# Attention outputs made transposed, a step later, and scaled by spread inverses

## The chip, the cores and the metric

The kernel runs on one core of a Trainium2 chip. What is measured is the time on the device of one execution, in microseconds (us); a lower time is better. TensorE is written PE in the profile, its weight loads PEld, VectorE is DVE, ScalarE is ACT, GpSimd is POOL, and SyncE, which issues most transfers, is SP.

## The reference

Eight sequences of 512 tokens by 128 features go through two residual layers. Layer 0 is a state space filter (16 states, 256 inner channels) with a gate and feed-forward part behind it, beside a two-of-eight expert layer chosen for each sequence. Layer 1 is causal attention with 16 heads of 64, beside an expert layer in which each token picks two of eight experts. The part that matters here is the attention:

```
q, k = _rope(q, k)
scores = jnp.einsum('bhqd,bhkd->bhqk', q, k)
scores = jnp.where(causal[None, None], -jnp.inf, scores)
attn = jax.nn.softmax(scores / math.sqrt(DK), axis=-1)
out = jnp.einsum('bhqk,bhkd->bhqd', attn, v)
out = out.transpose(0, 2, 1, 3).reshape(Bx, Sx, H * DV)
return out @ wo.T + bo
```

where v carries a bias bv. All data are float32.

## The kernel before

Each engine has an instruction list of its own; they meet through semaphores. The eight sequences go through in laps. A lap of sequence b has a `phase_1` (the filter's tail and layer 0 of b, the token experts of b-1, the front of the filter of b+1) and a `phase_2` (the attention of b, and beside it 13 of the 16 states of the filter's scan of b+1). The last sequence's `phase_2` has no scan beside it, since there is no b+1.

`phase_2` has 32 steps. The heads are taken in eight pairs j, and each pair in four steps t = 0 to 3, one for each block of 128 query rows; step s = 4j + t treats tiles n = 2s and 2s+1, the pair's two heads. A query block t sees t+1 key blocks. For each tile the work goes from engine to engine:

- PE, `scores` (L1038, with the causal mask added by L1041). The two heads' keys and queries lie in partitions 0 to 63 and 64 to 127. A step makes the scores of step s+2.
- DVE, `largest` (L1856): the row maxima. ACT, `exponentials` (L1341): exp and the row sums.
- PE, `turn` (L1049): transposes the exponentials into the bank G[2], t+1 blocks. There is one such bank, so the next turn waits for the copy out of it.
- ACT, `copy_turned` (L1349): copies them to PT, of which there are two, one for each head.
- PE, `weigh_values` (L1064): stationary is the turned block (128 by 128), moving are 64 columns of V; the output in G[3] has queries in partitions. Each float32 matmul shows as two weight loads and two matmuls.

Per pair, in step t = 0 of the next pair, DVE's `divide` inverts the row sums (L1861) and multiplies all of G[3] by them (L1868). In step t = 1 (`OUT_STEP`) PE's `turn_out` (L1073) transposes the result in four blocks into the bank FC, and ACT's `copy_out` (L1359) adds bv and puts it where `project_out` (L1081) reads it at the end of the phase. The last pair's `turn_out` stands behind the first seven `project_out`.

PE's order in a step is: turn(2s), weigh(2s-1), the scan's two selections (L796 and L800, `PICKS_AT`), turn(2s+1), a guest that uses FC (a projection L1026, `turn_out`, or rows to be turned), and then scores(s+2) and weigh(2s). DVE's order is: the maxima of step s+1, `divide` if t = 0, the scan's parts of this step (`PIECES`: a product L1550, a scan L1555, a product L1577), and a projection's rotation (L1850).

Of the kernel before, what the change touches and what calls it, by code (L numbers as in the profile page):

```python
# [35 lines left out]
P = 128  # L36
# [87 lines left out]
def build(nc, xT, weights, vecs, conv_rows, dt_w, a_log, moe, experts,  # L124
          row_biases, cos, sin, identity, causal, row_of, in_u_w, outT):
    ctx = ExitStack()
    with ctx:
# [77 lines left out]
        def reg(k):  # L205
# [10 lines left out]
        PT = REG[:, 16:18, :]  # L216
# [31 lines left out]
        s_alog = ctx.enter_context(nc.semaphore("alog_exp"))  # L248
# [81 lines left out]
        ot_mm = signal("ot_mm", PAIRS)  # L330
        ot_copy = signal("ot_copy", PAIRS)
# [48 lines left out]
                 d1_mm, d2_mm, lg_mm, wb_mm, e1_mm, e2_mm, v_mm, pj_mm, sc_mm, pt_mm, pv_mm, ot_mm, wo_mm, gl_mm,  # L380
                 xtok_mm, rank_mm, xt_mm, gg_mm, ug_mm, dn_mm, yt_mm] + [n.by_pe for n in norms]
        by_act = [biased, u_silu, r_silu, soft, da_exp, qsq_d, ksq_d, q_gelu, g_act, d1_gelu, rt_act,
                  e1_gelu, v_copy, p_exp, pt_copy, ot_copy, gt_act, sl_act, xtok_c, xt_copy, yo_copy] + [n.s_square for n in norms]
# [113 lines left out]
        for s_ in range(STEPS):  # L497
            j_, t_ = s_ // TILES, s_ % TILES
            if s_ < 2:
                guest[s_] = (("proj", 2 + s_), (biased, 3 + s_))  # L500
            if t_ in PROJECT_AT and j_ + 2 < PAIRS:
                m_ = 2 * (j_ + 2) + PROJECT_AT.index(t_)
                guest[s_] = (("proj", m_), (biased, m_ + 1))
            if t_ == OUT_STEP and j_:
                guest[s_] = (("out", j_ - 1), (ot_copy, j_))
# [179 lines left out]
        def _(pe):  # L685
# [366 lines left out]
            def weigh_values(b, n):  # L1052
                j, i = n // PER_PAIR, n % PER_PAIR
                h, t = tile_of(n)
                pe.wait_ge(pt_copy.sem, pt_copy.at(b, n + 1))
                if i == 0 and j:

                    pe.wait_ge(o_d.sem, o_d.at(b, j))
                elif i == 0:
# [8 lines left out]
            def turn_out(b, j):  # L1068

                pe.wait_ge(o_d.sem, o_d.at(b, j + 1))  # L1070
                bank = take(b, ("out", j))
                for t in range(TILES):
                    mm = pe.transpose(bank[:, t * P:(t + 1) * P], O[:, t * P:(t + 1) * P], ident[:, :])  # L1073
                mm.then_inc(ot_mm.sem, 1)

            def project_out(b, j):
                if j == 0:

                    pe.wait_ge(p_exp.sem, p_exp.at(b))
                pe.wait_ge(ot_copy.sem, ot_copy.at(b, j + 1))  # L1080
                pe.matmul(G[4][:, :], w("wo", j * D), ot_slot(j), start=j == 0, stop=j == PAIRS - 1,  # L1081
                          skip_group_check=True).then_inc(wo_mm.sem, 1)
# [7 lines left out]
            def attention_end(b, following):  # L1090
                project_out(b, PAIRS - 1)

                pe.wait_ge(p_exp.sem, p_exp.at(b))
                pe.wait_ge(ot_copy.sem, ot_copy.at(b))
                pe.wait_ge(gt_d.sem, gt_d.at(b))
# [4 lines left out]
            def phase_2(b, f, t):  # L1100
# [17 lines left out]
                for s in range(STEPS):  # L1118
# [3 lines left out]
                    if s:  # L1122
                        weigh_values(b, 2 * s - 1)
# [10 lines left out]
                    if key[0] == "proj":  # L1134
                        project(b, key[1])
                    elif key[0] == "out":
                        turn_out(b, key[1])
# [30 lines left out]
            def late():  # L1168

                pe.wait_ge(s_late, n_late)  # L1170
                pe.wait_ge(s_made, 17)
# [9 lines left out]
        def _(act):  # L1181
# [109 lines left out]
            def token_use(b, part, i, following):  # L1291
# [6 lines left out]
                if i >= 2:  # L1298
                    act.wait_ge(hh_d.sem, hh_d.at(b, i - 1))
                act.activation(SL[:, i % 2, :], G[2 * (i % 2)][:, :], ACT.Tanh, scale=0.5).then_inc(sl_act.sem, 1)  # L1300
# [43 lines left out]
            def copy_turned(b, n):  # L1344
                width = (tile_of(n)[1] + 1) * P
                act.wait_ge(pt_mm.sem, pt_mm.at(b, n + 1))
                if n >= 2:
                    act.wait_ge(pv_mm.sem, pv_mm.at(b, n - 1))
                act.activation(PT[:, n % 2, 0:width], G[2][:, 0:width], ACT.Copy).then_inc(pt_copy.sem, 1)  # L1349

            def copy_out(b, j):
                if j == 0:

                    act.wait_ge(wo_mm.sem, wo_mm.at(b - 1))
                    act.wait_ge(dn_mm.sem, dn_mm.at(b - 1))
                    act.wait_ge(e2_mm.sem, e2_mm.at(b))
                    act.wait_ge(yf_d.sem, yf_d.at(b))
                act.wait_ge(ot_mm.sem, ot_mm.at(b, j + 1))
                act.activation(ot_slot(j), ring_bank[("out", j)][:, :], ACT.Identity, bias=vec("bv", j)).then_inc(ot_copy.sem, 1)  # L1359
# [8 lines left out]
            def phase_2(b, f, t):  # L1368
# [10 lines left out]
                for s in range(STEPS):  # L1379
# [13 lines left out]
                    if s + 1 < STEPS:  # L1393
                        exponentials(b, 2 * s + 3, f)
                    if key[0] == "proj":
                        add_bias(b, key[1])
                    elif key[0] == "out":
                        copy_out(b, key[1])
# [20 lines left out]
        def _(dve):  # L1419
# [439 lines left out]
            def divide(b, j):  # L1859
                dve.wait_ge(p_exp.sem, p_exp.at(b, PER_PAIR * (j + 1)))  # L1860
                dve.reciprocal(rows[:, j % 2, 1, :], rows[:, j % 2, 0, :]).then_inc(rec_d.sem, 1)  # L1861
                if j:

                    dve.wait_ge(ot_mm.sem, ot_mm.at(b, j))
                dve.wait_ge(pv_mm.sem, pv_mm.at(b, PER_PAIR * (j + 1)))
                dve.wait_ge(rec_d.sem, rec_d.at(b, j + 1))

                dve.tensor_tensor(O.rearrange("p (t h d) -> p t h d", t=TILES, h=2),  # L1868
                                  G[3][:, :].rearrange("p (t h d) -> p t h d", t=TILES, h=2),
                                  rows[:, j % 2, 1, :].rearrange("p (h t) -> p t h", h=2).unsqueeze(3).to_broadcast([P, TILES, 2, DK]),  # L1870
                                  ALU.mult).then_inc(o_d.sem, 1)
# [12 lines left out]
            def phase_2(b, f, t):  # L1884
# [13 lines left out]
                for s in range(STEPS):  # L1898
# [5 lines left out]
                    if t_ == 0 and j:  # L1904
                        divide(b, j - 1)
# [13 lines left out]
                    elif key[0] == "return" and t is not None:  # L1919
                        give_back(t, ring_bank[key])  # L1920
                divide(b, PAIRS - 1)
# [12 lines left out]
            def late():  # L1934
# [6 lines left out]
                dve.wait_ge(s_made, 17)  # L1941
# [233 lines left out]
```

## Time and profile before

| | |
|---|---|
| median of 3 runs | 2456.86 us (2449.41 to 2474.56) |
| the profiled execution | 2465.26 us, its span 2463.1 us |
| PE, DVE, ACT, POOL busy | 83%, 67%, 48%, 39% of the span |
| mean granted clock of PE | 0.913 |

The profile is of one execution. The busy share of PE contains the modelled tail of each matmul, so a busy PE can still be one that waits.

### The profile page before, as it was taken

Reading aid. Unit: us, or ns where it says so; the run is one execution under the profiler, and the core shown is the slowest. Engines: PE = TensorE matmul, PEld = TensorE weight load, DVE = VectorE, ACT = ScalarE, POOL = GpSimd, SP = SyncE. Lnnn points to the kernel's source line nnn. Section 1 sums busy time; section 2 is a strip of 40 time slices with the busy share of each in tenths; the row PEclk is TensorE's granted clock in tenths of the full one; section 3 lists DMA queues with packets and bytes.
Section 4 is the critical chain, followed back from the end, with each engine's and each line's share of the span. In section 5 each row is a group of like instructions: output and inputs, shape, how many; then the busy total and the mean of one; then the engine's idle time right before and its main releaser. Section 6 shows DMA issues by size and latency. Waiting matters only on the chain.

```text
span 2463.1 us, 38971 instructions
## 1 busy us (share of the span) xinstructions
PE 2051.6 (83%) x11640; PEld 1426.4 (58%) x11640; DVE 1661.6 (67%) x2938; ACT 1186.9 (48%) x2703; POOL 955.0 (39%) x580
## 2 busy tenths in 40 slices
PE   4267888987899888998899888998889878888985
PEld 1043556755666556665566656665656646666664
DVE  4945886578855888558965688558876688645431
ACT  2223564345634466345643466345653456424631
POOL 1420572037710476007920287105940177203501
PEclk8577899998999899999999999999999999989997
DMA  2000012321213112321123112221123211232233
GB/s 105 0 18 0 35 51 70 115 70 41 85 65 111 57 44 69 105 99 44 57 71 115 68 48 81 78 98 62 46 74 106 87 44 60 72 125 71 71 107 119
DMA packets 82452, 175.06 MB, mean 71 GB/s; under 512 B 11448, under 2 KB 42560, under 8 KB 81984
## 3 DMA queue, kind: packets, MB, share of 16 engines
q1 hardware_dynamic: 78144, 164.05, 19.4%
q0 software_dynamic: 4096, 8.40, 1.1%
q8 instruction: 107, 1.75, 0.3%
q14 instruction: 105, 0.86, 0.1%
HBM read 123.71 MB, written 15.14 MB: 56 GB/s over the span
## 4 chain that ended last, share of the span: by engine, by line
PE 49%; DVE 21%; issue 14%; ACT 6%; POOL 5%; DMA 3%; SPq 1%; DVEq 1%; ACTq 0%; POOLq 0%
PE G L1064 7%; DVE HS L1555 6%; PE G L1049 5%; PE FM L1038 3%; PE G L953 3%; PE FC L1026 3%; PE G L942 3%; PE G L936 3%; DMA MW<-moe 2%; ACT REG L1349 2%; PE G L1081 2%; PE FM L906 2%; DVE maxes L1856 2%; DVE D L1550 2%; POOL Y L1984 2%
## 5 line engine op out<-in xcount | busy, mean ns | idle before, releaser
L1064 PEld LDWEIGHTS G<-REG 128*128 128x128 f32 x2560 | 347.5, 198 | 59.5 <-issue 49.7
L1555 DVE TENSOR_TENSOR_SCAN HS<-DA,D 128x1024 f32<-128x1024 f32 x128 | 359.3, 2807 | 19.4 <-ACT DA L1226 18.9
L1064 PE MATMUL G<-REG 128*128 128x64 f32 x2560 | 356.0, 272 | 3.2 <-DVE REG L1868 3.2
L1049 PE MATMUL G<-ident,REG 128*128 128x128 f32 x1280 | 241.7, 289 | 113.3 <-ACT REG L1349 111.1
L1984 POOL TENSOR_TENSOR Y<-Y,HC 128x1024 f32<-128x1024 f32 x114 | 271.1, 2378 | 163.4 <-DVE HC L1577 120.8
L1349 ACT ACTIVATE REG<-G 128x128 f32<-128x128 f32 (+3 forms) x512 | 222.9, 435 | 110.6 <-PE G L1049 105.0
L1995 POOL TENSOR_TENSOR REG<-REG,cos_t 128x512 f32<-128x512 f32 x128 | 170.8, 1334 | 257.1 <-ACT REG L1325 257.0
L1049 PEld LDWEIGHTS G<-ident,REG 128*128 128x128 f32 x1280 | 148.7, 149 | 162.1 <-issue 127.1
L1341 ACT ACTIVATE REG<-G,maxes 128x128 f32<-128x128 f32 (+3 forms) x384 | 195.4, 509 | 82.1 <-DVE maxes L1856 82.1
L1998 POOL TENSOR_TENSOR REG<-REG 128x512 f32<-128x512 f32 x128 | 207.1, 1618 | 56.9 <-DMA REG<-ROT 49.0
L1038 PE MATMUL G<-REG 64*128 64x128 f32 (+3 forms) x768 | 217.4, 482 | 9.8 <-POOL REG L1998 8.8
L1226 ACT ACTIVATE DA<-DELTA,a_neg 128x511 f32<-128x511 f32 x256 | 180.1, 718 | 46.8 <-DVE HS L1555 46.7
L1856 DVE TENSOR_REDUCE maxes<-G 128x1 f32<-128x128 f32 (+3 forms) x384 | 166.0, 458 | 14.2 <-PE G L1041 13.1
L936 PE MATMUL G<-XGT,MW 128*128 128x128 f32 x960 | 139.4, 292 | 29.1 <-DMA MW<-moe 28.9
L936 PEld LDWEIGHTS G<-XGT,MW 128*128 128x128 f32 x960 | 129.6, 204 | 56.2 <-issue 49.4
L1962 POOL TENSOR_SCALAR Y<-US,V_ 128x512 f32<-128x512 f32 x16 | 24.8, 1560 | 351.6 <-ACT US L1200 351.6
L1550 DVE TENSOR_TENSOR D<-DU,FB 128x1024 f32<-128x1024 f32 x114 | 138.2, 1213 | 23.6 <-PE FB L796 21.0
L1289 ACT ACTIVATE YO<-G 128x128 f32<-128x128 f32 x120 | 33.1, 276 | 247.6 <-PE G L953 247.6
L1968 POOL TENSOR_TENSOR DU<-DELTA,US 128x1024 f32<-128x1024 f32 x8 | 18.8, 2346 | 333.6 <-DVE DELTA L1542 333.6
L942 PEld LDWEIGHTS G<-XGT,MW 128*128 128x128 f32 x960 | 129.4, 204 | 24.0 <-issue 24.0
L1325 ACT ACTIVATE REG<-FC,V_ 128x512 f32<-128x512 f32 x112 | 77.0, 687 | 134.0 <-DVE ROT L1850 132.7
L953 PE MATMUL G<-MW,HC 128*128 128x128 f32 x960 | 140.0, 294 | 1.1 <-DVE HC L1732 1.1
(291 smaller groups left out, 4267.1 us busy)
## 6 DMA issues: line engine op xcount, KB each, us to landing
MW<-moe SPq DMA_DIRECT2D x120, 768.0 KB, 4.2
REG<-ROT SPq DMA_DIRECT2D x256, 128.0 KB
EW<-experts SPq DMA_DIRECT2D x16, 514.5 KB, 4.6
XG<-x_rows SPq DMA_DIRECT2D x8, 960.0 KB, 5.4
y_rows<-YO SPq DMA_DIRECT2D x120, 64.0 KB, 1.5
X<-xT SPq DMA_DIRECT2D x8, 256.0 KB, 6.2
W<-weights SPq DMA_DIRECT2D x1, 2048.0 KB, 9.4
REG<-xT SPq DMA_DIRECT2D x8, 256.0 KB, 2.9
```

Of the source, the lines that this page charges most:

```text
L936: mm = pe.matmul(G[2 * (i % 2)][:, c * P:(c + 1) * P], MW[:, i % SLOTS, c * P:(c + 1) * P], XGT[:, i, :], start=True, stop=True)
L942: mm = pe.matmul(G[2 * (i % 2) + 1][:, c * P:(c + 1) * P], MW[:, i % SLOTS, at:at + P], XGT[:, i, :], start=True, stop=True)
L953: mm = pe.matmul(G[4][:, 0:D], HH[:, i % 4, c * P:(c + 1) * P], MW[:, i % SLOTS, 2 * HID + c * D:2 * HID + (c + 1) * D], start=c == 0, sto ...
L1038: pe.matmul(bank[:, 0:width], QK[lo:lo + DK, j % 2, 0, t * P:(t + 1) * P], QK[lo:lo + DK, j % 2, 1, 0:width], start=True, stop=False)
L1049: mm = pe.transpose(G[2][:, c * P:(c + 1) * P], PR[:, n % 2, c * P:(c + 1) * P], ident[:, :])
L1064: mm = pe.matmul(G[3][:, col:col + DK], PT[:, n % 2, c * P:(c + 1) * P], V[:, c, j * P + h * DK:j * P + (h + 1) * DK], start=c == 0, stop= ...
L1341: act.activation(PR[:, n % 2, 0:width], ring_bank[("score", n)][:, 0:width], ACT.Exp, bias=maxes[:, j % 2, at:at + 1], accum_out=rows[:, j ...
L1349: act.activation(PT[:, n % 2, 0:width], G[2][:, 0:width], ACT.Copy).then_inc(pt_copy.sem, 1)
L1555: dve.tensor_tensor_scan(HS[:, :, :].rearrange("p h s -> p (h s)"), DA[:, n % 2, :, :].rearrange("p h s -> p (h s)"), D1[:, :, :].rearrang ...
L1856: dve.tensor_reduce(maxes[:, j % 2, at:at + 1], ring_bank[("score", n)][:, 0:width], AX.X, ALU.max, negate=True).then_inc(nm_d.sem, 1)
L1984: pool.tensor_tensor(Y[:, :, :], Y[:, :, :], HC_EARLY if early else HC[:, n % 2, :, :], ALU.add).then_inc(y_add.sem, 1)
L1998: pool.tensor_tensor(rotated, rotated, REG[:, 8 + m % 2, :], ALU.add).then_inc(rope_d.sem, 1)
```

## The change

PE's `weigh_values` now makes the output transposed. Stationary are 64 columns of V, moving is the turned block with 128 columns, and the output of head h lies in partitions 64h to 64h+63 of G[3]. Both heads of a step are done together, alternating, one step later than the first was before: in step s behind turn(2s), the values of step s-1. PT has a second pair of buffers (SL, which is free in this phase). `turn_out` is replaced by `spread_inverse`: eight matmuls whose stationary operand is a column of inverses repeated 64 times and whose moving one is the identity, so that the inverses stand beside the transposed outputs; for the last pair it comes ahead of the `project_out`s. ACT copies G[3] to O in step t = 0 of the next pair, and DVE multiplies O by the spread inverses in step t = 1, right behind the maxima of that step and ahead of the scan's parts. The value bias goes through wo into bo once, in `late`.

```
-            def weigh_values(b, n):
...
-                col = t * P + h * DK
-                for c in range(t + 1):
-                    mm = pe.matmul(G[3][:, col:col + DK], PT[:, n % 2, c * P:(c + 1) * P],
-                                   V[:, c, j * P + h * DK:j * P + (h + 1) * DK], start=c == 0, stop=c == t)
-                mm.then_inc(pv_mm.sem, 1)
+            def weigh_values(b, s):
+                j, t = s // TILES, s % TILES
+                pe.wait_ge(pt_copy.sem, pt_copy.at(b, 2 * s + 2))
+                if t == 0 and j:
+                    pe.wait_ge(o_copy.sem, o_copy.at(b, j))
+                elif t == 0:
+                    pe.wait_ge(place_d.sem, place_d.at(b, 5))
+                for c in range(t + 1):
+                    for h in range(2):
+                        mm = pe.matmul(G[3][h * DK:(h + 1) * DK, t * P:(t + 1) * P], V[:, c, j * P + h * DK:j * P + (h + 1) * DK],
+                                       PT[s % 2][:, h, c * P:(c + 1) * P], start=c == 0, stop=c == t)
+                        if c == t:
+                            mm.then_inc(pv_mm.sem, 1)
+            def spread_inverse(b, j):
+                pe.wait_ge(rec_d.sem, rec_d.at(b, j + 1))
+                bank = take(b, ("out", j))
+                for t in range(TILES):
+                    for h in range(2):
+                        mm = pe.matmul(bank[h * DK:(h + 1) * DK, t * P:(t + 1) * P],
+                                       rows[:, j % 2, 1, h * TILES + t:h * TILES + t + 1].to_broadcast([P, DK]), ident[:, :],
+                                       start=True, stop=True)
+                mm.then_inc(rinv_mm.sem, 1)
...
                     turn(b, 2 * s)
                     if s:
-                        weigh_values(b, 2 * s - 1)
+                        weigh_values(b, s - 1)
...
-                    if t_ == 0 and s + 2 < STEPS:
+                    if s + 2 < STEPS:
                         scores(b, s + 2)
-                    weigh_values(b, 2 * s)
-                    if t_ and s + 2 < STEPS:
-                        scores(b, s + 2)
-                weigh_values(b, N_TILES - 1)
+                weigh_values(b, STEPS - 1)
+                spread_inverse(b, PAIRS - 1)
                 for j in range(PAIRS - 1):
                     project_out(b, j)
-                turn_out(b, PAIRS - 1)
...
+                for j in range(PAIRS):
+                    mm = pe.matmul(G[2][:, 0:1], w("wo", j * D), vec("bv", j), start=j == 0, stop=j == PAIRS - 1)
...
             def copy_out(b, j):
+                if j:
+                    act.wait_ge(o_d.sem, o_d.at(b, j))
+                act.wait_ge(pv_mm.sem, pv_mm.at(b, PER_PAIR * (j + 1)))
+                act.activation(O, G[3][:, :], ACT.Copy).then_inc(o_copy.sem, 1)
...
+            def divide(b, j):
...
+                dve.wait_ge(o_copy.sem, o_copy.at(b, j + 1))
+                dve.wait_ge(rinv_mm.sem, rinv_mm.at(b, j + 1))
+                dve.tensor_tensor(ot_slot(j), O, ring_bank["out", j][:, :], ALU.mult).then_inc(o_d.sem, 1)
...
                     if t_ == 0 and j:
-                        divide(b, j - 1)
+                        invert_sums(b, j - 1)
+                    if key[0] == "out":
+                        divide(b, key[1])
```

## Rows read from the trace of the kernel before

**Rows 1.** The page: busy time, and the chain that ended last by engine.

```profile
PE 2051.6 (83%) x11640; PEld 1426.4 (58%) x11640; DVE 1661.6 (67%) x2938; ACT 1186.9 (48%) x2703; POOL 955.0 (39%) x580
...
PE 49%; DVE 21%; issue 14%; ACT 6%; POOL 5%; DMA 3%; SPq 1%; DVEq 1%; ACTq 0%; POOLq 0%
```

**Rows 2.** Windows: a lap's attention with scan, and the last lap's without.

```profile
core 0: us, PE busy (x) PEld busy (x) DVE busy (x) ACT busy (x) POOL busy (x), PEclk, DMA share, GB/s
1130.00:1267.00 137.00, 115.11 (x774) 81.96 (x773) 119.78 (x147) 89.99 (x244) 102.40 (x61) 0.96 0.17 58
...
2286.00:2362.00 76.00, 71.10 (x523) 53.36 (x522) 31.38 (x66) 53.89 (x153) 34.52 (x30) 1.00 0.22 76
```

**Rows 3.** The waits in 1130 to 1267: who for whom, total, times, longest.

```profile
PE G L1049 <- ACT REG L1349: 16.2, 20, 3.4
...
DVE maxes L1856 <- PE FM L1041: 4.0, 5, 0.9
DVE REG L1868 <- PE G L1064: 3.3, 6, 1.8
```

**Rows 4.** The chain that ended last, 1130 to 1267, shares by line.

```profile
by line: issue 23.5%; PE G L1064 12.1%; DVE HS L1555 8.4%; PE G L1049 7.7%; DVE maxes L1856 5.0%; ACT REG L1349 4.8%; PE FM L1038 4.5%; PE FC L1026 4.4%; DVE HC L1577 3.4%; DVE place_i L1832 2.6%; PE G L1038 2.0%; DVE ROT L1850 1.9%; POOL R
```

**Rows 5.** The timeline, PE and PEld, around a group of scores.

```profile
1251.40 0.97 PEld L1064 LDWEIGHTS G<-REG 128*128 128x128 f32 x8
...
1252.45 0.48 PE L1038 MATMUL FM<-REG 64*128 64x256 f32 x1
1252.45 0.48 PE L1038 MATMUL G<-REG 64*128 64x256 f32 x1
...
1252.77 0.38 PE L1038 MATMUL FM<-REG 64*128 64x256 f32 x1
...
1253.08 0.10 PEld L1041 LDWEIGHTS FM<-causal_bf,ident_bf 128*128 128x128 bf16 x1 [0.33 <-issue]
```

**Rows 6.** The timeline at a matmul that fills eight columns of the array.

```profile
466.82 0.75 PEld L953 LDWEIGHTS G<-MW,HC 128*128 128x128 f32 x6
467.69 0.10 PEld L765 LDWEIGHTS FM<-US,W 128*8 128x8 f32 x2
```

**Rows 7.** The chain in order of time in the last lap (start, us, what).

```profile
2287.40 0.39 ACT REG L1349
2287.80 0.14 issue
...
2288.78 0.39 PE G L1064 x4
...
2292.84 0.61 PE G L1064 x6
...
2294.57 0.61 ACT REG L1349
...
2296.80 0.84 PE G L1064 x8
...
2298.60 0.84 PE G L1064 x8
```

**Rows 8.** The timeline at two `turn_out`s, DVE's maxima beside them.

```profile
1242.27 1.01 DVE L1856 TENSOR_REDUCE maxes<-G 128x1 f32<-128x384 f32 x2
1243.32 0.47 PEld L1073 LDWEIGHTS FC<-ident,REG 128*128 128x128 f32 x4
...
1257.37 1.01 DVE L1856 TENSOR_REDUCE maxes<-G 128x1 f32<-128x384 f32 x2
1257.93 0.47 PEld L1073 LDWEIGHTS FC<-ident,REG 128*128 128x128 f32 x4
```

**Rows 9.** The timeline at the end of an attention phase, and L714's loads.

```profile
1266.99 0.69 DVE L1868 TENSOR_TENSOR REG<-G,rows 128x512 f32<-128x512 f32 x1 [1.84 <-PE G L1064]
...
1274.07 0.30 PEld L1081 LDWEIGHTS G<-REG,W 128*128 128x128 f32 x2 [1.01 <-ACT REG L1359]
...
1298.13 1.87 PEld L714 LDWEIGHTS FM<-ones,REG 128*128 128x128 f32 x16
```

More of the change, by code:

```diff
@@ L215, in build @@
         PR = REG[:, 14:16, :]
-        PT = REG[:, 16:18, :]
+        PT = (REG[:, 16:18, :], SL)
         O, OT = reg(18), reg(19)
@@ L329, in build @@
         o_d = signal("o_d", PAIRS)
-        ot_mm = signal("ot_mm", PAIRS)
-        ot_copy = signal("ot_copy", PAIRS)
+        rinv_mm = signal("rinv_mm", PAIRS)
+        o_copy = signal("o_copy", PAIRS)
         wo_mm = signal("wo_mm", PAIRS)
@@ L504, in build @@
             if t_ == OUT_STEP and j_:
-                guest[s_] = (("out", j_ - 1), (ot_copy, j_))
+                guest[s_] = (("out", j_ - 1), (o_d, j_))
             if s_ == RETURN_STEP:
@@ L1136, in phase_2 @@
                     elif key[0] == "out":
-                        turn_out(b, key[1])
+                        spread_inverse(b, key[1])
                     elif key[0] == "turn":
@@ L1299, in token_use @@
                     act.wait_ge(hh_d.sem, hh_d.at(b, i - 1))
+                else:
+                    act.wait_ge(pv_mm.sem, pv_mm.at(b))
                 act.activation(SL[:, i % 2, :], G[2 * (i % 2)][:, :], ACT.Tanh, scale=0.5).then_inc(sl_act.sem, 1)
@@ L1346, in copy_turned @@
                 act.wait_ge(pt_mm.sem, pt_mm.at(b, n + 1))
-                if n >= 2:
-                    act.wait_ge(pv_mm.sem, pv_mm.at(b, n - 1))
-                act.activation(PT[:, n % 2, 0:width], G[2][:, 0:width], ACT.Copy).then_inc(pt_copy.sem, 1)
-            def copy_out(b, j):
[L1352 to L1359, printed above, removed]
+                if n >= 4:
+                    act.wait_ge(pv_mm.sem, pv_mm.at(b, n - 3))
+                elif n >= 2:
+                    act.wait_ge(hh_d.sem, hh_d.at(b - 1))
+                act.activation(PT[n // 2 % 2][:, n % 2, 0:width], G[2][:, 0:width], ACT.Copy).then_inc(pt_copy.sem, 1)
+            def copy_out(b, j):
+                if j:
+                    act.wait_ge(o_d.sem, o_d.at(b, j))
+                act.wait_ge(pv_mm.sem, pv_mm.at(b, PER_PAIR * (j + 1)))
+                act.activation(O, G[3][:, :], ACT.Copy).then_inc(o_copy.sem, 1)
             def early_scan(f, n, part, b):
@@ L1394, in phase_2 @@
                         exponentials(b, 2 * s + 3, f)
+                    if s and s % TILES == 0:
+                        copy_out(b, s // TILES - 1)
                     if key[0] == "proj":
                         add_bias(b, key[1])
-                    elif key[0] == "out":
-                        copy_out(b, key[1])
                     elif key[0] == "turn":
@@ L1857, in largest, with invert_sums @@
                                   negate=True).then_inc(nm_d.sem, 1)
-            def divide(b, j):
+            def invert_sums(b, j):
                 dve.wait_ge(p_exp.sem, p_exp.at(b, PER_PAIR * (j + 1)))
                 dve.reciprocal(rows[:, j % 2, 1, :], rows[:, j % 2, 0, :]).then_inc(rec_d.sem, 1)
[L1862 to L1871, printed above, removed]
+            def divide(b, j):
+                if j == 0:
+                    dve.wait_ge(wo_mm.sem, wo_mm.at(b - 1))
+                    dve.wait_ge(dn_mm.sem, dn_mm.at(b - 1))
+                    dve.wait_ge(e2_mm.sem, e2_mm.at(b))
+                dve.wait_ge(o_copy.sem, o_copy.at(b, j + 1))
+                dve.wait_ge(rinv_mm.sem, rinv_mm.at(b, j + 1))
+                dve.tensor_tensor(ot_slot(j), O, ring_bank["out", j][:, :], ALU.mult).then_inc(o_d.sem, 1)
             def attention_end(b, following):
@@ L1920, in phase_2 @@
                         give_back(t, ring_bank[key])
+                invert_sums(b, PAIRS - 1)
                 divide(b, PAIRS - 1)
@@ L1940, in late @@
                 dve.tensor_scalar(q_b, q_b, DK ** -0.5, None, ALU.mult).then_inc(s_made, 1)
-                dve.wait_ge(s_made, 17)
+                dve.wait_ge(s_alog, 3)
+                dve.tensor_tensor(vec("bo"), vec("bo"), G[2][:, 0:1], ALU.add).then_inc(s_made, 1)
+                dve.wait_ge(s_made, 18)
             def finish(t):
```

23 lines of the change are left out of this document (7 added, 16 removed).

## The prediction

> **What bounds the kernel now.** I read the page first [rows 1]: PE is busy 83% and carries 49% of the chain that ended last, DVE 67% and 21%. That is an average, so next I cut out one lap's attention by windows [rows 2]. In its 137 us DVE is busy 119.8 and PE 115.1. The last lap's attention, which has no scan beside it, is a different machine: in 76 us PE is busy 71.1 and DVE only 31.4. So PE sets the last lap, and the seven laps with a scan are bound by PE and DVE together, each waiting for the other at times. The list of waits says at what [rows 3]: PE's turns wait 16.2 us for ACT's copies in 20 places, DVE's maxima wait 4.0 us for scores, and `divide` waits 3.3 us for the values. The chain of such a lap gives the matmuls of the values (L1064) 12.1%, or 16.6 us of the 137 [rows 4]. Those matmuls take 0.11 us apiece (0.97 us for a run of eight loads [rows 5]) and a lap has 320 (16 heads, ten blocks, two matmuls each), so 35 us of PE; 16.6 of 35 is 0.47, and with that share of PE's time I convert a saving on PE into one of the lap.
>
> **The change part by part.**
>
> *The values.* The count of matmuls stays 320 a lap. Moving 128 columns instead of 64 costs nothing by itself: four loads and matmuls of L1073, which move 128 columns, take 0.47 us, which is the same 0.11 apiece [rows 8]. The gain can only be that the two heads' matmuls, which fill different columns of the array, go at once. No row of this kernel shows that. The nearest rows are the scores, whose heads fill different rows of the array: both start at 1252.45, and the second of a head starts 0.32 later [rows 5]. If columns behave as rows do, a step with n matmuls takes n/2 places of 0.11 us; if not, n. The bounds are far apart, and I take the half, since the scores are the nearest row.
>
> *Changing the shape.* The same rows price it. The eight loads from 1251.40 would be followed by a ninth at 1252.28 or so, and the first of the scores comes at 1252.45: 0.15 lost. The pair that starts at 1252.77 streams 256 columns in 0.21 (0.32 less a load of 0.11), ends at 1252.98, and the next load comes at 1253.08, 0.10 late and with nothing to cover it, another 0.05 [rows 5]. At L765, which fills eight columns, six loads from 466.82 should be followed at 467.48 and are at 467.69 [rows 6]: 0.21 lost, so partial columns pay it too. In and out cost 0.30 us, once a step.
>
> The Trainium skill, in "TensorEngine Tiling (Array Packing)", Key Properties, says both things: different tiles can load and multiply in parallel, and a change of the tiling mode drains the engine. The trace agrees with the second (the 0.10 to 0.21 above); with the first it agrees for rows and is silent for columns.
>
> *One pair of heads on PE, by the last lap's chain* [rows 7]. Between turn(2s) and turn(2s+1) PE must wait for ACT's copy: 0.39 us for t = 1 to 0.61 for t = 3 and 0.14 of passing on. In t = 0 it is the eight matmuls of the values that take longer, 0.84. These gaps are 0.55, 0.64, 0.75, 0.84 for t = 1, 2, 3, 0 (the copy of t = 2 lies between the two shown). After the change the gap holds the values of the whole step before: 2, 4, 6, 8 places of 0.11 and 0.30, so 0.52, 0.74, 0.96, 1.18. It grows by 0, 0.10, 0.21, 0.34: 0.65 us. Behind turn(2s+1) the second head's values go: 0.39, 0.61, 0.84 [rows 7] and 0.22 for t = 0, 2.06 us. What stands there still (scores, and a projection in two steps of four) is longer than the next copy, so I count no new wait; it costs up to 0.4 us in a step if ACT is late with it. `spread_inverse` has 16 matmuls in 8 places, 0.88, and a change of shape, 0.15 (its way out is shared with the scores behind it), where `turn_out` took 0.44: 0.6 more. Sum: 0.65 + 0.6 - 2.06 = -0.8 us for a pair, -6.5 us for a lap.
>
> *The end of the phase.* Before, the last `turn_out` and ACT's copy stand between the seventh `project_out` and the eighth, and PE waits 1.01 us for it [rows 9]. Now the spreading comes ahead of six microseconds of `project_out`, which cover ACT's copy and DVE's product. That takes 1.0 us off each lap.
>
> *DVE.* The product stays 0.69 us [rows 9] and one is made for each pair, so DVE has no less to do. The wait changes. Before, `divide` waits 3.3 us in a lap, of which 1.84 lie at the end beside `project_out` [rows 3, 9], so 1.5 on the way. After, DVE stands behind the maxima of step t = 1 until PE has come to the spreading in that same step and done it, and behind it wait the scan's parts, so the product with B or C that PE's selections and POOL's sums wait for. Two places show how DVE and PE stand there: the maxima end at 1243.28 and 1258.38, and `turn_out` begins at 1243.32 and 1257.93 [rows 8]. The spreading would end some 1.2 us behind that beginning (0.15, 0.88, the tail of the last matmul 0.17 or so), so DVE waits 1.2 and 0.8: 1.0 a pair, 7 in a lap, less the 1.5 that go: +5.5 us of waiting. What of it is paid runs from nothing (PE is quicker, DVE falls behind it and finds the inverses made) to all of it. I take a third, 1.8 us, because DVE's own lines that show on the chain (8.4, 5.0, 3.4, 2.6 and 1.9%) make 21% of it beside the 12.1% of the values alone [rows 4], and because the maxima's own wait for the scores, 4.0 us [rows 3], takes up part of a late start.
>
> *ACT, POOL, SP.* ACT copies G[3] as often as it copied FC before. It moves from t = 1 to t = 0 and stands behind the exponentials there; PE needs it a step later. No transfer is moved. The values wait for both copies of a step that is over, so nothing is queued behind them that isn't free already.
>
> *`late`.* Eight matmuls of one column show as sixteen, 1.87 us by L714's [rows 9], and one small operation on DVE: 2.2 us, once.
>
> *Sum.* A lap with a scan: 0.47 of -6.5 is -3.1, with -1.0 and +1.8 that is -2.3; seven of them -16.1. The last lap: -6.5 - 1.0 = -7.5. `late` +2.2. Together -21.4 of the profiled 2465.3 us, 0.87%. The profiled execution lies 0.3% above the median, 2456.86; the same share of that gives 2436 us.
>
> **The rivals.**
>
> *PE's saving is paid out in full.* If DVE's waits are all for PE's sake and shrink with it, each scan lap gains 7.5 us: 7 x 7.5 + 7.5 - 2.2 = 58 us, 2399. For it: DVE waits for scores and values at all. Against it: DVE is busy 119.8 of 137 us, so more than 17 us a lap isn't there for anyone.
>
> *DVE's wait takes it.* All 5.5 us of waiting are paid and PE's saving beside DVE is worth only the 1.0 at the end: 7 x 4.5 - 7.5 + 2.2 = +26 us, 2483. It decides from the point where PE reaches the spreading later than DVE ends its maxima; both rows seen have it so. Halfway lies no change, 2460.
>
> *The columns don't go at once (slower).* Then the gaps behind turn(2s) hold 4, 8, 12, 16 places and 0.30: 0.74, 1.18, 1.62, 2.06 against 0.55, 0.64, 0.75, 0.84, 2.8 us more; the spreading is 1.76 + 0.15 - 0.44 = 1.5 more; 2.06 are saved. That is +2.2 a pair and 17.8 a lap. The last lap: +16.8. A scan lap: 0.47 x 17.8 - 1.0 + a third of (7 x 1.9 - 1.5) = +11.3, seven +79. With `late` +98 us, 4%: 2555. For it speaks that each float32 stream reads 128 partitions, where each of the scores' reads 64; nothing in the trace shows two full streams at once.
>
> *Only the loads get in each other's way.* The two heads' matmuls overlap, and each load waits for the matmul before it, so that a place is 0.16 (0.11 and half of a 128-column load, 0.05). Twenty places in a pair's values and eight in the spreading add 1.4 us to the -0.8: +0.6 a pair and +4.8 a lap. The last lap: +3.8; a scan lap: 0.47 of 4.8, -1.0 and the third of DVE's wait, +1.8 to +2.2, together +3.2. With `late` +28 us, 2485. "TensorE: Matmul & The Clock Gate", What overlaps and what doesn't, of the Trainium skill says that a load overlaps a matmul in flight only where the row group differs, and here it doesn't. The trace speaks against it in the full shape: the eight loads of L1064 come at 0.11 with matmuls between them in the same rows [rows 5].
>
> **How the numbers follow.** A measurement of this kernel tells 1% from no change, 25 us. Chances: my sum with its unknowns, 2405 to 2465, 0.47; PE's saving in full, 2370 to 2405, 0.08; DVE's wait or the loads, 2465 to 2500, 0.20; the columns one after the other, 2500 to 2590, 0.25. From 2395 to 2545 hold some 0.8 of it. Faster by over 1% (below 2432) takes the second and a little over half of the first: 0.34. Slower by over 1% (above 2481) takes the last and a small part of the third: 0.30. The rest, 0.36, is within 1%.
>
> **What will show it.** In the profile after, L1064's successor for the two heads starts in pairs a few nanoseconds apart if the columns go at once, and a step with 16 of them takes 0.9 and not 1.8 us. The wait of DVE's product for the spreading is 1 us a pair. PE's turns wait far less for ACT's copies than the 16.2 us a lap of before. The last lap's attention is 7 us shorter, a scan lap's 2. The wait ahead of the eighth `project_out` is gone. I am wrong if the pairs don't start together, if a change of shape costs other than 0.15 us, or if the scan laps move otherwise than the sum of both engines' waits.

## The result, and the profile after

The changed kernel takes 2484.28 us (median of 20 runs, 2470.26 to 2501.34) where the kernel before takes 2461.58 us (median of 20 beside them). The ratio is 1.009, with a 95% interval of 1.0068 to 1.0112: it is slower by 0.9%, where I had forecast 0.9% faster. The profiled execution has a span of 2480.3 us at a granted clock of 0.906.

The page of the kernel after, its busy line and the chain by engine, which answer to [rows 1]:

```profile
PE 2036.6 (82%) x12424; PEld 1294.5 (52%) x12424; DVE 1612.0 (65%) x2939; ACT 1174.2 (47%) x2703; POOL 939.6 (38%) x580
...
PE 47%; DVE 19%; issue 17%; POOL 7%; ACT 6%; DMA 3%; SPq 1%; DVEq 0%; ACTq 0%; POOLq 0%
```

PE does less (2036.6 us for 2051.6), DVE too, and the kernel takes longer. So it waits more. The groups of instructions of the kernel after say where (busy, mean ns of one, idle time ahead of it and what ended it):

```profile
L1049 PE MATMUL G<-ident,REG 128*128 128x128 f32 x1280 | 245.6, 292 | 137.8 <-ACT SL L1361 79.0 <-ACT REG L1361 55.5 <-issue 0.6
L1564 DVE TENSOR_TENSOR_SCAN HS<-DA,D 128x1024 f32<-128x1024 f32 x128 | 330.1, 2579 | 14.5 <-ACT DA L1232 13.2
L1065 PE MATMUL G<-REG 128*64 128x128 f32 x1024 | 88.2, 294 | 23.6 <-ACT REG L1368 21.3 <-issue 1.0
L1880 DVE TENSOR_TENSOR EW<-REG,FC 128x512 f32<-128x512 f32 x32 | 22.0, 688 | 61.0 <-PE FC L1077 51.2 <-issue 9.8
L1880 DVE TENSOR_TENSOR MW<-REG,FC 128x512 f32<-128x512 f32 x24 | 16.5, 687 | 36.3 <-PE FC L1077 36.3
L1880 DVE TENSOR_TENSOR REG<-REG,FC 128x512 f32<-128x512 f32 x8 | 5.5, 687 | 17.9 <-PE FC L1077 17.9
```

Three readings. DVE's product (L1880) waits 61.0 + 36.3 + 17.9 = 115 us, where `divide` waited 28 in the run before (3.3 in the stretch of [rows 3]). PE's turns (L1049) wait 134.5 us for ACT's copies, where they waited 111.1 (16.2 in the stretch). And the first values of a pair wait 21.3 us for a copy that wasn't in that place before, ACT's of G[3] (L1368). One place of the timeline of the kernel after shows how they come about (start, duration, engine, line, idle time before):

```profile
889.68 0.60 ACT L1368 ACTIVATE REG<-G 128x512 f32<-128x512 f32 x1
889.82 1.22 DVE L1586 TENSOR_TENSOR HC<-HS,FB 128x1024 f32<-128x1024 f32 x1
890.42 0.44 PE L1065 MATMUL G<-REG 128*64 128x128 f32 x4 [0.53 <-ACT REG L1368]
890.96 1.02 DVE L1865 TENSOR_REDUCE maxes<-G 128x1 f32<-128x384 f32 x2
891.10 0.39 PE L796 MATMUL FB<-S,pick 96*128 96x512 bf16 x1 [0.24 <-DVE HC L1586]
891.33 0.38 PE L1049 MATMUL G<-ident,REG 128*128 128x128 f32 x2
891.64 1.09 PE L1077 MATMUL FC<-ident,rows 128*64 128x128 f32 x16
892.86 0.69 DVE L1880 TENSOR_TENSOR EW<-REG,FC 128x512 f32<-128x512 f32 x1 [0.88 <-PE FC L1077]
```

PE comes to the values at 889.9 and stands 0.53 us, since ACT copies G[3] behind the exponentials; then it stands for the scan's selection; the spreading begins at 891.64 and ends 1.1 us later. DVE ended its maxima at 891.98 and waits 0.88. This is one of the shortest of these waits. Over the seven laps with a scan they are 1.8 us a pair in the mean; the first pair of a lap waits 2.5 us or more, in two laps 4.1.

### The profile page after: what moved, and what is told of

The parts are those of the page before. It is cut to its first block, busy times and chain, and to the rows that moved or that the text cites. A ratio compares the mean times of both kernels' runs of the same rounds, so it can differ in the third digit from the quotient of the medians.

```text
span 2480.3 us, 40604 instructions
## 1 busy us (share of the span) xinstructions
PE 2036.6 (82%) x12424; PEld 1294.5 (52%) x12424; DVE 1612.0 (65%) x2939; ACT 1174.2 (47%) x2703; POOL 939.6 (38%) x580
## 3 DMA queue, kind: packets, MB, share of 16 engines
q8 instruction: 114, 1.87, 0.3%
## 4 chain that ended last, share of the span: by engine, by line
PE 47%; DVE 19%; issue 17%; POOL 7%; ACT 6%; DMA 3%; SPq 1%; DVEq 0%; ACTq 0%; POOLq 0%
DVE HS L1564 4%; PE G L1049 4%; PE G L1065 4%; DMA MW<-moe 3%; PE G L942 3%; PE G L936 2%; PE G L953 2%; PE FC L1077 2%; PE FC L1026 2%; PE G L1087 2%; POOL Y L1998 2%; PE FM L906 2%; PE FM L1038 2%; POOL REG L2012 2%; POOL REG L2009 2%
## 5 line engine op out<-in xcount | busy, mean ns | idle before, releaser
L1049 PE MATMUL G<-ident,REG 128*128 128x128 f32 x1280 | 245.6, 292 | 137.8 <-ACT SL L1361 79.0
L1564 DVE TENSOR_TENSOR_SCAN HS<-DA,D 128x1024 f32<-128x1024 f32 x128 | 330.1, 2579 | 14.5 <-ACT DA L1232 13.2
L1049 PEld LDWEIGHTS G<-ident,REG 128*128 128x128 f32 x1280 | 150.4, 148 | 183.3 <-issue 130.6
L2012 POOL TENSOR_TENSOR REG<-REG 128x512 f32<-128x512 f32 x128 | 185.5, 1449 | 59.9 <-DMA REG<-ROT 52.6
L1361 ACT ACTIVATE SL<-G 128x256 f32<-128x256 f32 (+1 forms) x256 | 126.5, 494 | 43.9 <-PE G L1049 41.4
L1361 ACT ACTIVATE REG<-G 128x128 f32<-128x128 f32 (+1 forms) x256 | 97.7, 382 | 94.6 <-PE G L1049 92.7
L953 PEld LDWEIGHTS G<-MW,HC 128*128 128x128 f32 x960 | 134.2, 213 | 14.7 <-issue 13.9
```

The costliest lines, as they stand in the source:

```text
L953: mm = pe.matmul(G[4][:, 0:D], HH[:, i % 4, c * P:(c + 1) * P], MW[:, i % SLOTS, 2 * HID + c * D:2 * HID + (c + 1) * D], start=c == 0, sto ...
L1049: mm = pe.transpose(G[2][:, c * P:(c + 1) * P], PR[:, n % 2, c * P:(c + 1) * P], ident[:, :])
L1361: act.activation(PT[n // 2 % 2][:, n % 2, 0:width], G[2][:, 0:width], ACT.Copy).then_inc(pt_copy.sem, 1)
L1564: dve.tensor_tensor_scan(HS[:, :, :].rearrange("p h s -> p (h s)"), DA[:, n % 2, :, :].rearrange("p h s -> p (h s)"), D1[:, :, :].rearrang ...
L2012: pool.tensor_tensor(rotated, rotated, REG[:, 8 + m % 2, :], ALU.add).then_inc(rope_d.sem, 1)
```

## The experiments

All times are ratios to the kernel before, run beside each. The kernel after stands at 1.009. Differences in us are differences of these ratios times 2462 us. The kernel before took 2462 to 2470 us beside the experiments, so where an expectation below gives a time, the ratio and not the bare time decides.

**Where DVE's product stands.** The product moves behind the scan's parts of its step:

```
-                    if key[0] == "out":
-                        divide(b, key[1])
...
                     if f is not None:
                         for n, part in PIECES[s]:
                             front_step(f, n, part)
+                    if key[0] == "out":
+                        divide(b, key[1])
```

> The kernel after, with DVE's product of a pair moved behind the scan's parts of step t = 1. Three theories share the 22 us that the kernel after is slower than before. A, DVE's wait: DVE stands at the product 105 us in the whole run and the scan's parts stand behind it. Then the wait here falls below 50 us and the time to about 2460 us, that of before. B, the cost on PE: sixteen matmuls and two changes of shape a pair, and nothing of the wait is paid. Then the wait falls but the time stays between 2475 and 2490 us. C, ACT's queue: the turns and the values wait for ACT's copies (134 and 21 us), and DVE's place changes nothing: 2475 to 2490 us too, with those two waits as before. Against A alone speaks one thing: the projection of step t = 2 writes the bank that the product frees, so PE may wait for a later product (up to 1 us a pair, some 50 us in all), and the time then stays near 2484.

Measured: 0.9952 (0.9926 to 0.9978), so 1.4%, 34 us, less than the kernel after. The wait at the product is 34 us in place of 115, and PE waits 7 us for the product at its projections. Theory A holds: 81 us less waiting go with 34 us less time, a share of 0.42. The share is not the price of the wait alone, since the turns wait 17 us less and DVE's scans take 27 us more here (their lengths are compared further down).

**Where PE's spreading stands.** It goes from behind turn(2s+1) to behind turn(2s) of the same step, ahead of the values:

```
                     turn(b, 2 * s)
+                    if key[0] == "out":
+                        spread_inverse(b, key[1])
                     if s:
                         weigh_values(b, s - 1)
...
-                    elif key[0] == "out":
-                        spread_inverse(b, key[1])
```

> The kernel after, with the spreading of the inverses moved on PE from behind turn(2s+1) to right behind turn(2s) in step t = 1, ahead of the values, so some 2 to 3 us earlier. A, DVE's wait: it falls by 1.5 us or more at each of 49 products, by over 60 us in all, and the time falls to about 2460 us. B, the cost on PE: PE does the same matmuls, so 2475 to 2490 us. C, ACT's queue: the spreading now covers PE's waits for the copy of G[3] (21 us) and of turn(2s), so those fall by 15 us or more, and the time falls by as much even if DVE's wait weren't paid: 2465 to 2475 us.

Measured: 0.9832 (0.9794 to 0.9871), 2433.24 us: 2.6%, 64 us, less than the kernel after, and 1.7% faster than before, which took 2470.29 us beside it. It is the best version that computes everything. The groups of this kernel:

```profile
L1049 PE MATMUL G<-ident,REG 128*128 128x128 f32 x1280 | 243.5, 291 | 106.4 <-ACT SL L1361 62.7 <-ACT REG L1361 40.3 <-ACT REG L1350 0.2
L1065 PE MATMUL G<-REG 128*64 128x128 f32 x1024 | 87.4, 293 | 0.7
```

Both A and C come out: DVE's wait is 48 us, the wait for the copy of G[3] is gone (the spreading fills it), and the turns wait 31 us less. The same matmuls in another place take off more than the whole loss, so B, that the loss is the cost on PE, is refuted. That the spreading costs PE something is another matter; the run with two of the sixteen, below, prices it.

**DVE's wait by itself, first try.** DVE multiplies by another table and doesn't wait:

```
-                dve.wait_ge(rinv_mm.sem, rinv_mm.at(b, j + 1))
-                dve.tensor_tensor(ot_slot(j), O, ring_bank["out", j][:, :], ALU.mult).then_inc(o_d.sem, 1)
+                dve.tensor_tensor(ot_slot(j), O, sin_t[:, :], ALU.mult).then_inc(o_d.sem, 1)
```

> The kernel after, where DVE multiplies the copied outputs by the table of sines in SBUF in place of the spread inverses and doesn't wait for PE there; PE still spreads them. The outputs are not divided by the sums of their exponentials. It prices the wait for PE by itself. A: without the wait the scan laps lose all that they had gained by it, 2455 us or less (a third of the 105 us of waiting, or more). B and C: 2475 to 2490 us. What stands there may be taken up by the wait for the scores or the copy of G[3] behind it; then the wait at the product goes and DVE's other waits rise by most of it.

Measured: 1.0032 (1.0011 to 1.0053), 0.6% or 14 us less than the kernel after. That is neither A's 29 us or more nor the nothing of B and C, and the trace says why the run answers another question. Its view of that line (duration ns minimum, median, maximum):

```profile
L1879 DVE TENSOR_TENSOR EW<-REG,sin_t x32: 682/1118/4115, 296.9 to 2330.4; 128x512 f32<-128x512 f32 x32
L1879 DVE TENSOR_TENSOR MW<-REG,sin_t x24: 682/2139/4099, 363.6 to 2368.8; 128x512 f32<-128x512 f32 x24
```

The product, 0.69 us with one operand in PSUM, takes up to 4.1 us with both in SBUF. I had changed two things at once.

> As the run without DVE's wait, and PE does two of the sixteen matmuls that spread the inverses. It leaves the change of shape and takes 0.77 us of PE's time from each of 64 pairs, 49 us in all. The outputs are not divided by the sums of their exponentials. A: within 5 us of the run without the wait in the scan laps, 6 us less in the last lap: 2445 to 2455 us. B, the cost on PE: 25 to 49 us less than the run without the wait. C: as A, no more than 10 us less.

In the same version PE does only two of the sixteen (`for t in range(1)`). Measured: 0.9958 (0.9936 to 0.998), 0.74% or 18 us less than the one above, for 49 us of PE's time: a share of 0.37. It lies between A's 11 (5 and the last lap's 6) and B's 25, so the sixteen matmuls are not free, though they are not what makes the change slow.

**DVE's wait by itself, again.** DVE reads the bank FC as a guest left it, and PE writes its sixteen matmuls into a part of G[3] that is overwritten later (G[1] for the last pair). The outputs are not scaled by the inverses:

```
-                dve.wait_ge(rinv_mm.sem, rinv_mm.at(b, j + 1))
+                for of, k in ring_free["out", j]:
+                    if of is not o_d:
+                        dve.wait_ge(of.sem, of.at(b, k))
...
-                bank = take(b, ("out", j))
+                take(b, ("out", j))
+                bank = G[3] if j < PAIRS - 1 else G[1]
...
-                        mm = pe.matmul(bank[h * DK:(h + 1) * DK, t * P:(t + 1) * P],
+                        mm = pe.matmul(bank[h * DK:(h + 1) * DK, (2 + t % 2) * P:(3 + t % 2) * P],
```

> The run without DVE's wait used a table in SBUF, and the product then took 1.07 to 2.26 us in place of 0.69, which hid what was asked. Here DVE multiplies by what the bank FC last held, a read of PSUM as in the kernel after, and PE writes the same sixteen matmuls into a part of another bank that is overwritten later; DVE does not wait for them. The outputs are not divided by the sums of their exponentials. A: the wait of 105 us is gone but for the copies at the ends, the product takes 0.69 us, and the time falls by 34 us or more against the kernel after: 2450 us or less. If the wait is not what costs (B, C): 2475 to 2490 us.

Measured: 0.9927 (0.9899 to 0.9955), 1.6% or 40 us less than the kernel after. The product takes 0.68 us, and its wait, now for ACT, is 20 us in place of 115. So 95 us less waiting of DVE go with 40 us less time, again 0.42. PE's turns wait far less as well:

```profile
L1049 PE MATMUL G<-ident,REG 128*128 128x128 f32 x1280 | 243.0, 290 | 80.2 <-ACT SL L1362 51.5 <-ACT REG L1362 26.2 <-ACT REG L1351 0.2
```

That is 77.7 us for ACT's copies, where the kernel after has 134.5 and the kernel before 111.1. The turns' longer wait in the kernel after goes with DVE's wait: ACT's exponentials, which PE turns, wait 79 us for DVE's maxima here and 115 us in the kernel after.

**ACT's copy of G[3]** goes one instruction earlier:

```
+                    if s and s % TILES == 0:
+                        copy_out(b, s // TILES - 1)
                     if s + 1 < STEPS:
                         exponentials(b, 2 * s + 3, f)
-                    if s and s % TILES == 0:
-                        copy_out(b, s // TILES - 1)
```

> The kernel after, with ACT's copy of G[3] one instruction earlier, ahead of the second exponentials of step t = 0. C, ACT's queue: PE's wait for that copy at the first values of a pair, 21 us in all, goes, and the time falls by 10 to 20 us. A, DVE's wait: PE reaches the spreading up to 0.4 us earlier, so DVE's wait falls by 10 to 20 of its 105 us, and the time by 5 to 10 us. Against both: the exponentials, which both PE's next turn and the reciprocal wait for, come 0.6 us later in each pair, and the time stays within 5 us of the kernel after.

Measured: 1.0014 (0.9988 to 1.004), 0.75% or 19 us less. The wait for the copy falls from 21.3 to 4.8 us, DVE's only from 115 to 106. C holds for this wait. DVE's scans take 9 us less in this kernel, so some of the 19 may be theirs. The two gains, 40 and 19 us, make 59; the early spreading, which takes away most of both, gained 64.

**The order alone.** The kernel before with its own matmuls, and the values of both heads one step late (with the second buffers for the turned blocks):

```
                     turn(b, 2 * s)
                     if s:
+                        weigh_values(b, 2 * s - 2)
                         weigh_values(b, 2 * s - 1)
...
-                    if t_ == 0 and s + 2 < STEPS:
-                        scores(b, s + 2)
-                    weigh_values(b, 2 * s)
-                    if t_ and s + 2 < STEPS:
+                    if s + 2 < STEPS:
                         scores(b, s + 2)
```

> The kernel before, with its own matmuls (turned outputs, one head after the other, the product ahead of turn_out), where the values of both heads of a step go one step late behind turn(2s) and the copies have a second pair of buffers, as in the kernel after. It prices the order alone. If the late, bunched values are what costs (theory C: turns and G[3] wait longer for ACT), it is slower than before by 15 us or more, 2475 us or above. If the wait for the spreading is what costs (A), it is within 10 us of before, 2452 to 2472 us. By the lengths of the gaps behind turn(2s), which would hold 4 to 16 places of 0.11 us, PE does not save anything here, so no gain is expected from either.

Measured: 1.0104 (1.0063 to 1.0144), slower by as much as the whole change. But the reason isn't the one that I had written for it: its turns wait 102 us for ACT, less than before. What rises is `divide`'s wait for the last values, from 27.4 to 70.3 us, since both heads' values of step t = 3 now stand behind turn(2s) of t = 0, where DVE asks for them. By the trace it is DVE's wait once more, at another instruction; no run of this order without that wait was made.

**Both moves at once.**

> Both moves at once: the spreading right behind turn(2s), and DVE's product behind the scan's parts of its step. Each alone took time off the kernel after: 34 us and 64 us by the ratios. If they take away the same wait (A), the wait at the product goes from 48 us to the 20 at the phases' ends and the time stays within 8 us of the early spreading alone, 2425 to 2440 us. If each takes away something of its own, it is 2415 us or less. If a late product now holds back the projection of step t = 2, which writes the same bank (7 us of waiting with the product behind), it is above 2440 us.

Measured: 1.003 (0.9994 to 1.0067), 2.0% or 48 us worse than the early spreading alone, though the wait at the product is 20.6 us. A new cause had to be found. The timeline of this kernel, DVE's scan, GpSimd beside it, and PE:

```profile
911.12 6.19 DVE L1564 TENSOR_TENSOR_SCAN HS<-DA,D 128x1024 f32<-128x1024 f32 x1
...
911.58 2.35 POOL L1998 TENSOR_TENSOR Y<-Y,HC 128x1024 f32<-128x1024 f32 x1
913.89 1.26 POOL L2009 TENSOR_TENSOR REG<-REG,cos_t 128x512 f32<-128x512 f32 x1
915.31 3.06 POOL L2012 TENSOR_TENSOR REG<-REG 128x512 f32<-128x512 f32 x1 [0.16 <-POOL REG L2009]
...
918.99 0.30 PE L1049 MATMUL G<-ident,REG 128*128 128x128 f32 x1 [2.80 <-ACT REG L1361]
```

The scan, 2.3 us by itself, takes 6.19 where GpSimd has a sum of 2.35 us and a product of 1.26 in hand, both on SBUF, and the last of GpSimd's three takes 3.06 in place of 1.27. PE stands 2.8 us behind it. In this kernel pair 4 of a lap takes 16.6 us without such a meeting and 21.5 with it; from the first turn to the last, the laps with a scan take 132 or 140 us, but for the first with 137. The Trainium skill, "SBUF — State Buffer", Who interferes with whom, says that a DVE instruction with two SBUF inputs contends with a GpSimd instruction that reads SBUF, and that the second to issue is blocked. The trace agrees in which pairs of operations meet. As to the order, 50 scans of this kernel take over 2.6 us, and 45 of them start while one of GpSimd's sums or products already runs, which agrees; the one shown is of the other five, where the scan starts first, at 911.12, and is stretched even so. GpSimd's spans are rough, so these five decide nothing.

**Light GpSimd.** Four kernels (before, after, early spreading, both moves) where those sums and products of GpSimd touch 64 columns in place of 1024 or 512 (14 of the 128 sums keep their width). The other columns are left out, so the outputs are not the reference's:

```
+                w_ = S if early else 32
-                pool.tensor_tensor(Y[:, :, :], Y[:, :, :], ...
+                pool.tensor_tensor(Y[:, :, 0:w_], Y[:, :, 0:w_], ...
-                pool.tensor_tensor(rotated, rotated, cos_t[:, :], ALU.mult)
+                pool.tensor_tensor(rotated[:, 0:64], rotated[:, 0:64], cos_t[:, 0:64], ALU.mult)
...
```

> The kernel before, where GpSimd's sum into Y (2.36 us) and its two products and sums of the rotary embedding (1.27 us each) touch 64 of their 1024 or 512 columns, as many instructions and the same waits; so those sums are left out for the other columns. It asks what the stretched scans are worth: in the kernel before, DVE's scans take 2.3 us alone and 4 to 6.4 us where such an operation of GpSimd runs beside them, 65 us more in all. Theory P (the stretches, and which pairs they fall on, decide the differences of some 5 us between laps): all 112 scans of the attention laps take 2.3 us, the laps are alike within 1 us, and the time falls by 45 us or more. Rival: the scans are stretched by something else (DMA, ACT), and stay between 2.3 and 6 us; the time falls by no more than the 10 us for which PE waits for GpSimd.

> The kernel after with the same light GpSimd. P: scans of 2.3 us, even laps. Against the light kernel before: the kernel after had 37 us of stretched scans where before had 65 and was yet 22 us slower; if DVE's wait of 1.6 us a pair is simply paid, it is slower than the light before by 20 to 50 us. If the wait matters only where it moves the scan to GpSimd's operation, the two are within 10 us of each other, or after is the faster by up to 20.

> The kernel after with the early spreading and the light GpSimd. The early spreading gained 64 us on the kernel after. If that was PE's and DVE's waits, it is again 40 us or more faster than the light after. If half of it was the luck of where scans and GpSimd's operations met, it gains 15 to 35 us here.

> Early spreading, late product, and the light GpSimd. With GpSimd as it was, the late product made the early spreading 48 us slower, with stretched scans of 79 us against 47. P: that loss was the stretches, so here it is within 8 us of the light early spreading. Rival: the loss is in the waits of the products with B and C for PE's selections (64 us against 31), which come later behind a late PE; then it stays 25 us or more slower.

Measured, in that order: 0.9801 (0.9768 to 0.9833), 0.9918 (0.9888 to 0.9949), 0.9581 (0.9549 to 0.9613), 0.9583 (0.9548 to 0.9617). The scans of the light kernel before and of both moves:

```profile
L1555 DVE TENSOR_TENSOR_SCAN HS<-DA,D 128x1024 f32<-128x1024 f32 x128 | 297.4, 2324 | 19.8 <-ACT DA L1226 16.6 <-DVE D L1550 1.9 <-issue 0.6
```
```profile
L1564 DVE TENSOR_TENSOR_SCAN HS<-DA,D 128x1024 f32<-128x1024 f32 x128 | 297.7, 2326 | 14.2 <-ACT DA L1232 11.9 <-DVE D L1559 1.7
```

With light GpSimd the 128 scans take 297 us in every kernel. Against that, the heavy ones lose 62 us to the meetings in before (359.3), 33 in after, 43 with the early spreading (339.8) and 75 with both moves (372.0). The others stand between: 358 us of scans with the product behind, 338 without the wait, 321 with the copy ahead, 354 with the order alone. The loss of both moves is gone (0.9583 beside 0.9581), and the rival falls: the products with B and C still wait 51 us for PE's selections where they wait 34 with the early spreading alone, and that costs nothing. The light kernels shorten GpSimd's own operations too, so they price the long operations as a whole, of which the meetings are the part that the scans show. The kernel after stays slower than before, by 1.2% or 29 us: it isn't the meetings that made it so, and it even had fewer. I had expected 45 us or more from taking them away in the kernel before; 49 us came. The laps were not alike within 1 us (127 to 133 from the first turn to the last), so meetings are not all that varies.

These four also show that the share 0.42 is no constant. From the light after to the light early spreading 119 us of waits went (70 of DVE at the product, 25 for the copy of G[3], 24 of the turns) and the time fell by 83. From there to both moves the wait at the product fell by another 30 us, from 52.0 to 21.8, and the time did not change.

The windows of one lap's attention, of the light after and then of the light early spreading (us, busy time with instructions of PE, PEld, DVE, ACT, POOL, then the granted clock, DMA's share and GB/s):

```profile
1387.00:1544.00 157.00, 131.50 (x930) 73.85 (x929) 113.19 (x173) 96.50 (x258) 44.55 (x67) 0.93 0.17 55
```
```profile
1347.60:1490.00 142.40, 123.86 (x931) 70.85 (x930) 113.01 (x173) 95.28 (x257) 50.24 (x67) 0.99 0.18 60
```

The same matmuls take PE 131.5 us at a clock of 0.93 and 123.9 at 0.99, 7.6 of the 14.6 us between the two. This is the lap in which the two kernels differ most; in the fourth, from the first turn to the last `project_out`, both have PE busy for 116 us. The busy lines of the whole runs, of the light after and of the light early spreading:

```profile
PE 2023.9 (83%) x12424; PEld 1285.2 (53%) x12424; DVE 1549.6 (63%) x2939; ACT 1174.3 (48%) x2703; POOL 424.5 (17%) x580
```
```profile
PE 1991.3 (84%) x12424; PEld 1270.7 (54%) x12424; DVE 1548.8 (66%) x2939; ACT 1172.4 (50%) x2703; POOL 459.9 (19%) x580
```

The granted clock rises from 0.911 to 0.921 and PE's busy time falls by 33 us, of the 81 between the two spans. By the clock alone it would fall by 22 (an estimate, 2023.9 times 0.911 over 0.921). So a wait of PE goes with a lower clock too, and the two are paid together; that the waits are what lowers the clock is not shown apart.

## Why the prediction was wrong, step by step

*The columns go at once*: right. The timeline of the kernel after, the last turn ahead of a step of values and those values:

```profile
2314.60 0.14 PEld L1049 LDWEIGHTS G<-ident,REG 128*128 128x128 f32 x1
...
2314.86 0.85 PEld L1065 LDWEIGHTS G<-SL,REG 128*64 128x64 f32 x16
2314.86 1.09 PE L1065 MATMUL G<-SL,REG 128*64 128x128 f32 x16
```

Sixteen matmuls, eight of each head, take 1.09, where eight in the full shape take 0.97 [rows 5]. The rival of one after the other (2555) and that of loads in each other's way (2485, near the measured time for a wrong reason) fall with it.

*Changing the shape costs 0.15 in*: right. After the load at 2314.60 (0.11 apart in a run) the next would come at 2314.71 and comes at 2314.86.

*PE saves 6.5 us a lap by the last lap's chain*: wrong in size. From its first turn to the end of the last `project_out`, the last lap's attention went from 118.4 to 115.8 us, 2.6 in place of 7.5. And the order alone, with before's matmuls, has 115.8 too. Where I let the values set the gap behind turn(2s), ACT's copy does:

```profile
2350.72 0.61 PE L1049 MATMUL G<-ident,REG 128*128 128x128 f32 x4
2351.26 0.88 PE L1065 MATMUL G<-REG 128*64 128x128 f32 x12
2352.52 0.63 PE L1049 MATMUL G<-ident,REG 128*128 128x128 f32 x4 [0.39 <-ACT SL L1361]
```

Step t = 3: the copy of four blocks takes 0.60 us and starts 0.45 behind the turn's end, so the six places of values and the shape end 0.39 too early. What PE's saving is worth in a lap with a scan, 0.47 of 6.5 in the prediction, no run measured.

*The end of the phase, 1.0 us*: right. The wait ahead of the eighth `project_out`, 8.1 us over eight laps for its weight loads, is gone.

*No new wait, and the turns wait far less*: wrong, and the smaller of the two steps that failed. The turns wait 134.5 us where it was 111.1 (and 77.7 in the run without DVE's wait at the product, so this rise goes with that wait), and the copy of G[3], "behind the exponentials there; PE needs it a step later", comes too late for it: 21.3 us, a term that the sum has at nothing. The copy ahead prices it at 19.

*DVE waits 5.5 us a lap more, and a third of it is paid*: this is the step that failed most. Its direction, place and mechanism were right; the size was half, 1.0 us a pair where the laps with a scan show 1.8. The wait rose by 87 us in eight laps, 11 a lap. I had taken the place of `turn_out` in the kernel before for that of the spreading, but in the kernel after PE comes there later, since the waits for G[3] and for turn(2s+1) and the values lie ahead of it. The share paid, which I set at 0.33, came out at 0.42 in two kernels, whose scans took 27 and 8 us more than those of the kernel after. 0.42 of 11 is 4.6 in place of 1.8: over seven laps 20 us more than I had, with 19 for the copy of G[3] and 5 in the last lap 44 us, and -21 + 44 is +23; measured were +22.7. That it comes out so close is luck. The sum keeps the whole -21, with a saving on PE of which the last lap bore out a third; it leaves out that the scans of the kernel after were stretched by 29 us less than those of before; and the terms overlap in part (the copy ahead took 1.3 us off the last lap). What the runs do show without such a sum is that moving the spreading, which takes away both waits, gains 64 us, or 83 with light GpSimd, against a loss of 23, or 29.

*The rival "DVE's wait takes it"*, 2483 us, is what happened in kind, at 2484. The near number is again luck: it has all of 5.5 us paid, where 11 came and some 0.42 of it was paid, and it has nothing for the copy of G[3]. Its chance was put together with another at 0.20, since I judged the wait by two places of a lap [rows 8], both from the kernel before.

*`late`*: 3.4 us of PE's time for sixteen matmuls (0.21 apiece) in place of 1.87, once.

What stays open: how the 22.7 us divide between the lower clock and the waits in the kernel after itself, and what makes the laps of the light kernels differ by up to 6 us. The granted clock goes with it: in the light kernel before, the shortest such lap has 0.963 and the longest 0.917.

## What to carry to other kernels

When an instruction that waits is put ahead of long work of its engine, place it by when the other engine will get there in the new order, not where its predecessor stood in the old; then try the producer some instructions earlier before the consumer later. A gap that is filled with work has two lengths, that of the work and that of the copy it waits for: check which one sets it, step by step. And in a kernel where VectorE scans SBUF beside GpSimd, compare two orders only together with the busy time of the scan, since an order can lose 2% by where they meet.

## What the runs showed of the hardware

- Two float32 matmuls of 128 rows and 64 columns, in different column halves, go at once: 16 in 1.09 us with 128 columns moving.
- A DVE scan on two SBUF operands takes 2.3 us, and up to 6.4 beside GpSimd's elementwise operations on SBUF; a product of 0.69 us with a PSUM operand took up to 4.1 with both operands in SBUF. GpSimd's own operation was stretched too, from 1.27 to 3.06.
- Longer waits of PE go with a lower granted clock, enough to matter: the same 930 matmuls took 123.9 us at 0.99 and 131.5 at 0.93, and over the whole run PE's busy time was 1991.3 us at 0.921 and 2023.9 at 0.911.
